# New orders for all engines of six local-attention layers, with feed-forward and Newton work moved off GpSimd

## The reference

```python
for i in range(6):
    x = attn_layer(shift_tokens(x), Wqkv[i], q_scale[i], k_scale[i], Wo[i]) + x
    x = ffn_layer(shift_tokens(x), ln_g[i], ln_b[i], W1[i], b1[i], W2[i], b2[i]) + x
```

## Time and profile before

| | us |
|---|---|
| runs: median (lowest to highest) | 3357.97 (3355.26 to 3359.26) |
| the profiled execution's own time | 3364.21 |
| its span, first to last instruction | 3362.4 |
| PE busy (share of the span) | 3202.1 (95%) |
| POOL busy | 2972.7 (88%) |
| DVE busy | 2748.6 (82%) |
| ACT busy | 2741.9 (82%) |
| layers, from the first projection to the last instruction | 424.4 to 3362.4 |

### The profile page before, as it was taken

One profiled execution on the slowest core, in us unless ns is written; L12 is line 12 of the kernel. 1 busy time (PEld: TensorE's weight loads), 2 busy tenths in 40 slices (PEclk: granted clock), 3 DMA queues, 4 the chain that ended last, 5 costly groups with the idle time before them and its releaser, 6 DMA issues.

```text
span 3362.4 us, 158051 instructions
## 1 busy us (share of the span) xinstructions
PE 3202.1 (95%) x64570; PEld 2756.5 (82%) x64570; DVE 2748.6 (82%) x5172; ACT 2741.9 (82%) x4522; POOL 2972.7 (88%) x3540
## 2 busy tenths in 40 slices
PE   7999769999999999999999999999999999999997
PEld 5677448888888888888888888888888888888886
DVE  7777577888888888888888888888888888888886
ACT  4777457888888888888888888888888888888885
POOL 5687478999999999999999999999999999989995
PEclk9999889999999999999999999999999999999999
DMA  2000013222223222223222233222232222332222
GB/s 62 5 8 8 12 44 89 75 75 73 64 74 96 75 75 69 63 74 101 75 70 68 70 95 79 72 68 72 69 101 75 68 70 63 82 89 74 74 66 74
DMA packets 162047, 228.51 MB, mean 68 GB/s; under 512 B 42392, under 2 KB 60768, under 8 KB 161760
## 3 DMA queue, kind: packets, MB, share of 16 engines
q1 hardware_dynamic: 161888, 226.85, 25.2%
HBM read 21.00 MB, written 4.19 MB: 7 GB/s over the span
## 4 chain that ended last, share of the span: by engine, by line
PE 65%; POOL 12%; issue 7%; ACT 2%; DVE 1%; POOLq 0%; SPq 0%; DMA 0%; DVEq 0%; ACTq 0%
PE ring L1423 9%; PE ring L1382 8%; PE ring L1432 8%; PE proj L1373 7%; PE score L1401 6%; PE proj L1375 6%; PE proj L1374 6%; POOL by_cos L1253 4%; PE ring L1408 4%; PE ring L1485 3%; PE ring L1476 2%; POOL by_cos L1259 2%; POOL weightsb L1264 2%; PE ring L1477 2%; PE ring L1478 2%
## 5 line engine op out<-in xcount | busy, mean ns | idle before, releaser
L1253 POOL TENSOR_TENSOR by_cos<-by_cos,by_sin 128x1024 f32<-128x1024 f32 x384 | 915.4, 2384 | 20.2 <-DVE by_sin L1657 20.2
L1259 POOL TENSOR_TENSOR by_cos<-by_cos,norms 128x1024 f32<-128x1024 f32 x384 | 732.2, 1907 | 20.1
L1655 DVE TENSOR_TENSOR by_cos<-proj,turns 128x512 f32<-128x512 f32 x768 | 522.0, 680 | 186.7 <-PE ring L1382 118.2
L1373 PE MATMUL proj<-qkv_hi,xs_hib 128*128 128x512 f32 x1152 | 536.0, 465 | 31.3 <-ACT vb L1520 11.9
L1657 DVE TENSOR_TENSOR by_sin<-proj,turns 128x512 f32<-128x512 f32 x768 | 523.0, 681 | 0.0
L1541 ACT ACTIVATE squares<-proj 128x512 f32<-128x512 f32 x768 | 445.2, 593 | 28.3 <-PE proj L1375 16.3
L1661 DVE TENSOR_REDUCE sumsb<-squares 128x16 f32<-128x1024 f32 x384 | 464.3, 1209 | 0.0
L1375 PE MATMUL proj<-qkv_hi,xs_lob 128*128 128x512 f32 x1152 | 460.8, 400 | 0.0
L1374 PE MATMUL proj<-qkv_lo,xs_hib 128*128 128x512 f32 x1152 | 460.3, 400 | 0.5 <-issue 0.5
L1423 PEld LDWEIGHTS ring<-pTb,v_win 64*64 64x64 f32 x24576 | 382.1, 136 | 40.3 <-issue 37.2
L1382 PE MATMUL ring<-ident,by_cos 128*128 128x128 f32 x3072 | 411.5, 277 | 1.7 <-issue 1.5
(11 more groups left out here) (188 smaller groups left out, 7363.2 us busy)
## 6 DMA issues: line engine op xcount, KB each, us to landing
v_win<-vb SPq DMA_DIRECT2D x1152, 128.0 KB, 2.3
v_win<-vb SPq DMA_DIRECT2D x768, 64.0 KB, 2.0
in_qkv<-L_ffn_Wqkv SPq DMA_DIRECT2D x12, 768.0 KB
wo<-L_ffn_Wo SPq DMA_DIRECT2D x12, 256.0 KB, 4.0
x_tok<-L_attn_x SPq DMA_DIRECT2D x8, 256.0 KB, 4.7
residual<-x_tok SPq DMA_DIRECT2D x8, 256.0 KB, 2.0
in_w<-L_ffn_W SPq DMA_DIRECT2D x12, 170.5 KB
in_qkv<-residual SPq DMA_DIRECT2D x1, 1536.0 KB, 6.7
```

Source lines behind the costliest of these rows:

```text
L1253: nc.gpsimd.tensor_tensor(both, both, by_sin[:, j, :], ALU.add).then_inc(e[f"{w_}_added"].sem, 1)
L1259: nc.gpsimd.tensor_tensor(heads, heads, inverse, ALU.mult).then_inc(e[f"{w_}_ready"].sem, 1)
L1373: nc.tensor.matmul(out, xs_hi[:, tile], qkv_hi[:, cols], start=True, stop=False)
L1655: nc.vector.tensor_tensor(of_heads(by_cos[:, t % 2, j, cols]), heads, table(0), ALU.mult)
```

## The change

- All five lists (`CYCLE`, `NEXT_WEIGHTS`, `LAST`) have new orders, but for SP's. The cycle now begins after F4 with X:-2, and the v projection of a cycle's second tile stands in the next cycle (aPv:1, bPv:1).
- XL, the normalised x times gain plus shift, moves from POOL to DVE, with the same operands.
- Newton: ACT computes the square of the guess too, by a second Exp of double scale and bias, so POOL drops the first of its eight operations.
- The copy of the second feed-forward weights (NF) moves from POOL to ACT, behind the rounding of the first. One of the six `lo_` subtractions (lo_q1) moves from DVE to POOL.
- At the start POOL clears 32 of 256 columns per pair of heads of kT, and of v only 32 rows of the last tile (with 0 where 1 was), in a step of its own; all engines wait for `padded` 3 instead of 2.

```diff
 CYCLE = {
-    "PE": "aPq:2 Tq:0 bPq:2 Tk:0 X:-2 aPk:2 mean bPk:2 S:0 V:-2 Tq:1 aPv:2 bPv:2 X:-1 var aPq:3 bPq:3 spread "
-    "V:-1 Tk:1 aPk:3 bPk:3 GG S:1 AA aPv:3 bPv:3 W:-1 F4",
-    "Act": "IG:1 XSa:2 EV:1 EXP:-1 XF aQq:2 EQ:0 bQq:2 EK:0 MK:0 EX:-2 aQk:2 XSa:3 bQk:2 EO:-2 EQ:1 FSQ EV:2 "
-    "IG:2 EX:-1 aQq:3 EXP:0 bQq:3 XH EO:-1 EK:1 MK:1 aQk:3 bQk:3 GEL",
-    "DVE": "aCq:2 bCq:2 Rq:2 XC RS:-1 aCk:2 bCk:2 MX:0 Rk:2 FV SB:0 XM aCq:3 bCq:3 Rq:3 RS:0 aCk:3 bCk:3 Rk:3 "
-    "MX:1 AM SB:1 WX:-1 XN",
-    "Pool": "Mk:0 XSd:2 N:1 Mq:1 Ak:1 Mk:1 Aq:2 XSd:3 PN:-1 Ak:2 FP N:2 XL Xl Aq:3 Mq:2 PN:0",
+    "PE": "X:-2 aPv:1 mean bPv:1 Tk:0 Tq:0 aPq:2 bPq:2 V:-2 aPk:2 var S:0 bPk:2 spread Tk:1 aPv:2 X:-1 Tq:1 "
+    "bPv:2 V:-1 aPq:3 bPq:3 GG S:1 AA aPk:3 bPk:3 W:-1 F4",
+    "Act": "XSa:2 XF EX:-2 IG:1 EV:1 FSQ EK:0 aQq:2 bQq:2 EQ:0 MK:0 XSa:3 aQk:2 EO:-2 bQk:2 EK:1 XH EX:-1 EQ:1 "
+    "EV:2 EXP:0 MK:1 aQq:3 IG:2 bQq:3 EO:-1 GEL aQk:3 bQk:3 EXP:1",
+    "DVE": "XC RS:-1 aCq:2 Rq:2 bCq:2 FV aCk:2 XM bCk:2 XL MX:0 SB:0 Rk:2 RS:0 aCq:3 bCq:3 Rq:3 AM MX:1 SB:1 "
+    "aCk:3 WX:-1 bCk:3 XN Rk:3",
+    "Pool": "Mk:0 Aq:1 Ak:1 XSd:2 N:1 Mk:1 PN:-1 FP Mq:1 Aq:2 Xl XSd:3 Ak:2 PN:0 N:2 Mq:2",
     "SP": "VM:0 VM:1",
 }
 NEXT_WEIGHTS = {
-    "Act": {(-2, "aQq:3"): "hi_q0", (-2, "MK:1"): "hi_k0", (-2, "bQk:3"): "hi_k1", (-2, "GEL"): "hi_q1",
-          (-1, "EV:1"): "hi_v0", (-1, "EK:0"): "hi_v1"},
-    "DVE": {(-2, "XM"): "lo_q0", (-2, "AM"): "lo_q1", (-2, "WX:-1"): "lo_k1", (-2, "XN"): "lo_v0 lo_k0",
-          (-1, "aCk:2"): "lo_v1"},
-    "Pool": {(-2, "Aq:3"): "turn_0", (-1, "Mk:0"): "turn_1", (-1, "Mq:1"): "turn_2", (-1, "Mk:1"): "turn_3"},
+    "Act": {(-2, "aQq:3"): "hi_q0 hi_q1", (-2, "EXP:1"): "hi_k1 hi_k0", (-1, "XF"): "hi_v0",
+          (-1, "IG:1"): "hi_v1"},
+    "DVE": {(-2, "Rk:3"): "lo_q0", (-1, "XC"): "lo_k1", (-1, "RS:-1"): "lo_v0", (-1, "aCq:2"): "lo_k0",
+          (-1, "Rq:2"): "lo_v1"},
+    "Pool": {(-2, "Mq:2"): "turn_0", (-1, "Mk:0"): "turn_1", (-1, "XSd:2"): "turn_2 lo_q1",
+          (-1, "Mk:1"): "turn_3"},
 }
 LAST = {
-    "PE": "Tq:30 Y:0 mean:13 Y:1 X:28 Tk:30 V:28 S:30 var:13 X:29 spread:13 Y:2 V:29 Tq:31 W:29 Tk:31 GG:13 "
-    "AA:13 S:31 X:30 F4:13 V:30 Y:3 mean:14 var:14 X:31 Y:4 spread:14 V:31 GG:14 AA:14 Y:5 Y:6 W:31 F4:14 "
-    "mean:15 var:15 spread:15 Y:7 GG:15 AA:15 F4:15 Y:8",
...
+    "PE": "X:28 mean:13 aPv:31 Tk:30 bPv:31 Tq:30 V:28 Y:0 X:29 S:30 var:13 Tk:31 Y:1 spread:13 Tq:31 V:29 "
+    "GG:13 Y:2 S:31 AA:13 W:29 F4:13 X:30 mean:14 var:14 V:30 spread:14 X:31 Y:3 Y:4 V:31 GG:14 AA:14 Y:5 W:31 "
+    "F4:14 mean:15 var:15 Y:6 spread:15 GG:15 Y:7 AA:15 F4:15 Y:8",
...
-            steps += [(("NF",), 0, "", at // STEPS), (("NL",), 0, "", at // STEPS)]
+            steps.append((("NL",), 0, "", at // STEPS))
...
-            nc.gpsimd.memset(kT[:, :, :], 0.0)
+            nc.gpsimd.memset(kT[:, :, HS - WINDOW:HS], 0.0)
             nc.gpsimd.memset(sums[:, :, :, :, 1], L2_EPS2)
-            for n in range(TILES):
-                nc.gpsimd.memset(v[:, n, :, :, :], 1.0)
             nc.gpsimd.memset(hidden[:, FC - 1, :], 0.0).then_inc(padded, 1)
             pool.wait_ge(padded, 1)
             nc.gpsimd.memset(hidden[BIAS_ROW:BIAS_ROW + 1, FC - 1, :], 1.0).then_inc(padded, 1)
+            pool.wait_ge(padded, 2)
+            nc.gpsimd.memset(v[P - WINDOW:P, TILES - 1, :, :, :], 0.0).then_inc(padded, 1)
 
             def inverse_roots(t, when):
 
-                x, y, z = floors[:, t % 2, :], norms[:, t % 2, :], newton[:, :]
-                wait_tile(pool, "guess", t, when)
+                x, y, z = floors[:, t % 2, :], norms[:, t % 2, :], newton[:, t % 2, :]
+                wait_tile(pool, "guess", t, when, 2)
                 for n, limit in enumerate((c["three"], c["twelve"])):
                     if n:
+                        wait_tile(pool, "newton", t, when, 3)
+                        nc.gpsimd.tensor_tensor(z, y, y, ALU.mult).then_inc(e["newton"].sem, 1)
                         wait_tile(pool, "newton", t, when, 4)
-                    nc.gpsimd.tensor_tensor(z, y, y, ALU.mult).then_inc(e["newton"].sem, 1)
+                    nc.gpsimd.tensor_tensor(z, z, x, ALU.mult).then_inc(e["newton"].sem, 1)
                     wait_tile(pool, "newton", t, when, 4 * n + 1)
-                    nc.gpsimd.tensor_tensor(z, z, x, ALU.mult).then_inc(e["newton"].sem, 1)
+                    nc.gpsimd.tensor_tensor(z, limit[:, :], z, ALU.subtract).then_inc(e["newton"].sem, 1)
                     wait_tile(pool, "newton", t, when, 4 * n + 2)
-                    nc.gpsimd.tensor_tensor(z, limit[:, :], z, ALU.subtract).then_inc(e["newton"].sem, 1)
-                    wait_tile(pool, "newton", t, when, 4 * n + 3)
                     nc.gpsimd.tensor_tensor(y, y, z, ALU.mult).then_inc(e["newton" if n == 0 else "norm"].sem, 1)
...
-                elif kind == "XL":
+                elif kind == "Xl":
                     if b is None and p % STEPS == LAG:
                         pool.wait_ge(p_w1_lo, new + 1)
-                    wait_half(pool, "xn", when)
-                    pool.sem_inc(pool_ready, 1)
-                    nc.gpsimd.tensor_scalar(xb[:, :], xc[:, :], gain, shift, ALU.mult, ALU.add).then_inc(e["xb"].sem, 1)
-                elif kind == "Xl":
                     wait_half(pool, "xb", when)
                     wait_half(pool, "xn_hi", when)
                     nc.gpsimd.tensor_tensor(xn_lo[:, :], xb[:, :], xn_hi[:, :].bitcast(F32), ALU.subtract)\
...
-                elif kind == "NF":
-                    pool.wait_ge(loaded, all_loaded(new))
-                    wait_half(pool, "y_full", when, 0)
-                    nc.gpsimd.tensor_tensor(w2[:, :, :], in_w2[:, :, :], ones[:, :].unsqueeze(1).broadcast_to([P, FC, D]),
-                                            ALU.mult).then_inc(p_w2, 1)
...
                                          bias=c["guess_bias"][:, 0:1]).then_inc(e["guess"].sem, 1)
+                    nc.scalar.activation(newton[:, t % 2, :], floors[:, t % 2, :].bitcast(I32), ACT.Exp,
+                                         scale=2 * GUESS_SCALE, bias=c["square_bias"][:, 0:1]).then_inc(e["guess"].sem, 1)
...
                     wait_half(act, "up_full", when, 0)
                     copy(w1_hi[:, :, :], in_w1[:, :, :]).then_inc(p_w1_hi, 1)
+                    wait_half(act, "y_full", when, 0)
+                    copy(w2[:, :, :], in_w2[:, :, :]).then_inc(p_w2, 1)
...
+                elif kind == "XL":
+                    if b is None and p % STEPS == LAG:
+                        dve.wait_ge(p_col, new + 1)
+                    wait_half(dve, "xn", when)
+                    nc.vector.tensor_scalar(xb[:, :], xc[:, :], gain, shift, ALU.mult, ALU.add).then_inc(e["xb"].sem, 1)
```

More of the change, by code:

```diff
@@ L650, in other_constants @@
                 nc.vector.memset(c["guess_bias"][:, :], GUESS_BIAS)
+                nc.vector.memset(c["square_bias"][:, :], 2 * GUESS_BIAS)
                 nc.vector.memset(c["three"][:, :], 3.0 + GUESS_ERROR)
@@ L942, in layer_events @@
     return {
-        **each("xs_in", "xs_hi", "xs", "floor", "guess", "norm"), "newton": Events(sem("newton"), 7 * PER, LEAD + 1),
+        **each("xs_in", "xs_hi", "xs", "floor", "norm"), "guess": Events(sem("guess"), 2 * PER, LEAD + 1), "newton": Events(sem("newton"), 6 * PER, LEAD + 1),
         **each(*(f"{w}_{n}" for w in "qk" for n in ("sums", "added", "ready", "T_full", "T"))),
@@ L1016, in layers_stage @@
         sums, floors, norms = sb("sumsb", [P, 2, 2, H, 2]), sb("floors", [P, 2, 2 * H]), sb("norms", [P, 2, 2 * H])
-        newton, exp_table = sb("newton_b", [P, 2 * H]), sb("exp_table", [P, 1])
+        newton, exp_table = sb("newton_b", [P, 2, 2 * H]), sb("exp_table", [P, 1])
         by_cos, by_sin = sb("by_cos", [P, 2, 2, INNER]), sb("by_sin", [P, 2, INNER])
@@ L1207, in last_layer @@
                              residual[:, AT_ONCE * TILES:B * TILES, :]).then_inc(x_loaded, 16)
-            sp.wait_ge(padded, 2)
+            sp.wait_ge(padded, 3)
             run(sp, "SP", step, new_layer, last_layer)
@@ L1325, in step @@
                     pool.sem_inc(p_used, 1)
-            pool.wait_ge(padded, 2)
+            pool.wait_ge(padded, 3)
             pool.wait_ge(tables_loaded, 16 * 4)
@@ L1332, in _ @@
         def _(pe):
-            pe.wait_ge(padded, 2)
+            pe.wait_ge(padded, 3)
             user = {}
@@ L1516, in _ @@
         def _(act):
-            act.wait_ge(padded, 2)
+            act.wait_ge(padded, 3)
             def copy(out, in_):
@@ L1632, in _ @@
         def _(dve):
-            dve.wait_ge(padded, 2)
+            dve.wait_ge(padded, 3)
             def step(s_, t, token, when, b, new):
@@ L1764, in program @@
             "ones": sb("ones", [P, P]), "mean_of": sb("mean_of", [P, P]), "minus_half": sb("minus_half", [P, H]),
-            "guess_bias": sb("guess_bias", [P, 1]), "three": sb("three", [P, 2 * H]), "twelve": sb("twelve", [P, 2 * H]),
```

(1 more changed line is left out.)

## The result

The changed kernel takes 3390.34 us (median of 4 runs, 3387.01 to 3392.91), the kernel before 3358.61 (4 runs beside it, 3355.26 to 3366.34): a ratio of 1.0091 (95% interval 1.0079 to 1.0103). It is slower by 0.9%; forecast was 3338. The profiled execution took 3389.96, its span is 3387.8.

What follows compares the result with a forecast made beforehand. PE was taken to bound regular cycles, with waits at layer boundaries. Regular cycles 0, start -4, fill -1, boundaries -11, end -4 make -20: 3344 profiled, 3338 median; own range 3325 to 3351 (45%), 8-in-10 range 3314 to 3364.

Steps and rivals of the forecast that it cites:

- One row makes XL dearer: Regular cycles: POOL's addition can hold XL on DVE, 1.4 us beyond its own 0.4; PE's margins absorb it, cost 0.
- Rival 2: Regular cycles: held XL closes a loop as long as the cycle; 0.3 us more in each of 93, +28: 3366; 15%.
- PE's neighbours: Regular cycles: new neighbours of PE's matmuls change their cost by about 0, from -0.15 to +0.15 us a cycle.
- rival 3: Regular cycles: V in front of a projection costs 0.35 us, not 0.2; +0.15 a cycle, +14: 3352; 13%.
- Start: Kernel start: POOL clears less of kT and v, so PE's first matmul comes earlier; -4 us.
- Fill: Filling cycles: one ACT wait goes from each tile, another comes in; -1 us, between -4 and +3.
- Boundary, cycle 15: Layer boundary: PE's next projection waits on POOL's chain, 5.0 us late; sum 8.1 against 8.2, so 0, or -1.5.
- 3.1 for it: Layer boundary, cycle 15: 3.1 us added for PE's low clock behind a 2.9 us wait.
- Boundary, cycle 18: Layer boundary: POOL less loaded, spread waits some 1.1 us instead of 1.67; excess 2.6 becomes 1.2: -1.4.
- End: Kernel end: S:31 comes some 7 us earlier, V:31 gains 4; -4 us, between -8 and +2.

Runs made afterwards that it cites:

- e1: The changed kernel with XL alone put back on POOL, behind Aq:2 and ahead of Xl; 3331.77 us, ratio 0.9914 to the kernel before.
- e6: The kernel before, own orders, plus short clearing, second guess with shorter Newton, and second weights' copy on ACT; XL on POOL; 3342.20 us, ratio 0.9949.
- e5: As e1, but with Newton's eight operations, one guess, and the second weights' copy on POOL; short clearing stays; 3343.68 us, ratio 0.9958.
- e7: As e1, with turn_2 moved behind XSd:2 instead of ahead of it; 3323.25 us, ratio 0.9894 to the kernel before.
- e10: The changed kernel with XL still on DVE but behind MX:0, and turn_2 behind XSd:2; 3321.58 us, ratio 0.9881 to the kernel before.
- e8: The changed kernel with ACT's second guess IG:2 moved behind EO:-1; 3394.35 us, ratio 1.0104 to the kernel before.

## Why the prediction was wrong

**The step that failed** is the sentence behind "One row makes XL dearer": "MX:0, SB:0 and RS:0 then come later, but stay within the margins above". The hold and its size were there: XL was held (1.93 where 0.404 is its own time), and 0.4 + 1.4 was the estimate; the earlier trace rows had shown it. But the margins named are those of PE's waits, and RS:0 is in none of them. Its reciprocal releases PN:0, POOL's list runs from there to Aq:2 without slack, and XL can't end before Aq:2. For one cycle the sentence held: behind the boundary with the long low clock, where PE was late and XL met no addition (0.405), the next XL took 1.51 (estimate 1.8), AA didn't wait, and the next mean came after 29.15 (the last two rows below). But PN:0 came 29.70 after the one before it, XL then took 1.93, AA waited, and the cycle was the loop's 29.70, as in nearly all regular cycles of the trace: 0.5 to 0.6 more for 93 cycles, 47 to 56 us, where the forecast had 0. Timelines of DVE and PE there:

```profile
1909.76 1.51 DVE L1687 TENSOR_SCALAR xbb<-xcb,ffn_col 128x256 f32<-128x256 f32 x1
```

```profile
1897.91 0.59 PE L1447 MATMUL ring<-xfb,mean_of 128*128 128x256 f32 x2
1927.06 0.59 PE L1447 MATMUL ring<-xfb,mean_of 128*128 128x256 f32 x2
```

**Rival 2** had the sign, the place (AA waits for EO:-1 in each cycle, which was its sign under "What would show it") and the loop. Only its length was short: PN:0 to Aq:2 was put at 23.8 and is 24.08, the rest at 5.4 and is 5.62 with the two handovers of 0.15. So its price of 0.3 came out as 0.51 (0.60 against e1), its 3366 as 3390. The sentence against it, "when POOL drifts late, XL gets in ahead of Aq:2 and costs only 0.4", did not come true: PE and with it XM can't get ahead of a late POOL, as AA waits for EO:-1, which hangs on the same late SB:0. In 74 of 96 cases XL starts 0.6 behind Aq:2. The rule of the Trainium skill, "SBUF — State Buffer", section "Who interferes with whom", was quoted as speaking against this move; the traces agree with it (held 1.93, alone 0.404), and the weight given to it, 15%, was too small.

**PE's neighbours**, taken as 0: right. Without the hold the cycle is 29.10 against 29.19, -0.09, inside the -0.15 to +0.15. V ahead of a projection costs 0.20 (0.43 for its first matmul against 0.23), as chosen; rival 3's 0.35 is out.

**Start**, -4: right, by its own steps: from the clearing's begin to PE's first matmul it is 2.47 us, before 6.13, 3.7 less. (The time up to the first projection varies by more, 416.0 to 423.6 among the changed kernels, with what lies ahead of the clearing.) The rows after, to be read against the earlier trace rows; POOL's clearing, then PE's first matmul:

```profile
411.99 0.31 POOL L1224 MEMSET kTb<- 128x256 f32 x1 [3.22 <-POOLq L122]
...
413.05 0.95 POOL L1230 MEMSET vb<- 32x1024 f32 x1
```

```profile
414.46 0.63 PE L1488 MATMUL score<-mask_win,ident_bf 128*128 128x512 bf16 x1 [3.37 <-POOL vb L1230]
```

**Fill**, -1 with -4 as its end: mis-sized, -11.6. e6 against e5 shows that it is the new lists. In the two traces about 4 of it are fewer waits of PE up to the first "mean" (the idle times in the timelines sum to 23.6 before, 19.3 after, the first projection's own wait left out), and one v projection of some 1.4 is done after it. The rest wasn't followed up and stays open.

**Boundary, cycle 15**: the waits were placed partly right. Forecast were 1.4 for Tk:0, 1.0 for Tq:0 and 1.9 for XSd:2; measured 1.39 for AA, 1.70 for the mean (ACT's xfb) and 2.05 for XSd:2. These make 5.1; the forecast's three make 4.3, though its sum went on with 5.0. lo_q1 on POOL was put at 1.3 and took 1.72, XSd:2 0.91 instead of 0.45, both beside DVE's lo steps. The low clock was 6.7 us before and is 3.4 here (the windows above; 10.2 at one of the five), so "3.1 for it" was 1.4 too much at four of them. e7 and e10 show what stood in the sum and was not questioned: turn_2 ahead of XSd:2 is on the path, and nothing needs it there.

**Boundary, cycle 18**: spread's wait was to be 1.1 and is 0.89. In all a boundary gained 1.4 (forecast 2.2); with XL unheld, as assumed, 2.7 (e1).

**End**, -4: wrong, +2.1. S:31 came 3 us sooner, not 7 (20.5 behind the last full cycle's F4 instead of 23.6), and V:31 came 4 later. Part of it is the clock. Windows of the kernel after, same columns as above:

```profile
3345.00:3350.00 5.00, 3.73 (x83) 3.19 (x85) 3.39 (x9) 2.28 (x4) 2.91 (x3) 0.99 0.76 209
3350.00:3355.00 5.00, 4.49 (x85) 4.02 (x81) 1.38 (x4) 1.02 (x1) 1.90 (x2) 0.50 0.03 7
```

PE waits 1.27 for ACT's FSQ in the first of these, and works at 1.2 GHz in the second. e7 has the same list of PE and 1.00 throughout this stretch, and a tail of 67.4 instead of 70.4; e10, whose clock falls there as in after, has 70.3. So at full clock the new order gains 1, and the low clock takes some 3.

Without the hold the forecast of -20 would have been low: e1, which differs in XL alone, measured 29.1 us less than the kernel before, and its trace has -12.1 in the fill, -15.5 in the 80 cycles, and less than 1 in each of the other stretches.

## What to carry to other kernels

An operation moved from GpSimd to VectorE is priced by what GpSimd does at the moment it comes, not by its length: here 0.4 or 1.93 us, and one place later in the list decided between -1.1% and +0.9%. When a delay is found, don't only hold it against the waits of the bounding engine: follow it until it comes back to where it began, add up the whole loop, and compare it with the cycle. A margin absorbs a delay once; a loop that is longer than the cycle makes a new one each time, and moves PE's wait about (AA, or W:-1 in e8) without getting shorter. And a piece of work that nobody on the path needs yet belongs behind the step that PE waits for, not ahead of it: that was worth some 8 us (0.2%) in five places by the traces.

## What the hardware showed beyond that

- A held DVE operation doesn't pay its length again: in the change XL ends 0.15 behind POOL's addition (1181.20 after 1181.05). In e10 it starts 0.26 before that addition ends (1164.17, 1164.43), ends 0.14 behind it and takes 0.40 in all. So a start a quarter of a microsecond early was free.
- The clock at the boundary answered near-equal waits differently. With 1.83 to 1.85 (e1) it was at 1.2 GHz in two of five boundaries, once for 10.2 us and once for 3.4; with 0.40 to 0.46 (e7, e10) in none. About V:31, near the end, it fell in after and in e10, not in e7, which differs from e10 only in XL's engine. No forecast of single microseconds can rest on it there.
